# A graph network's sorting stage: node sums by wide matmuls, file copies by DMA, and all normed rows on ScalarE

## The reference

```python
x = _layernorm(x + _L0_gnn_ref(x, L0_gnn_W, L0_gnn_c, edge_index), axis=-1)
x = _layernorm(x + _L1_gnn_ref(x, src, dst, ...), axis=-1)
x = _layernorm(x + _L2_gnn_ref(x, edge_index, ...), axis=-1)
x = _layernorm(x + _L3_gnn_ref(x, edge_index, edge_attr_16, batch0, ...), axis=-1)
```

```python
f = h + EPS
f = f * CLIP / jnp.maximum(CLIP, _norm(f))
p = jnp.tanh(fn) * f / fn
Mp = p @ W
t = Mp * atan_norm / pn / sqrt_c
hh = jnp.tanh(sqrt_c * tn) / sqrt_c / tn * t
```

## Time and profile before

| | us |
|---|---|
| median of 3 runs | 8033.82 |
| lowest and highest | 8025.30, 8053.64 |
| the profiled execution | 8009.85 |
| its span in the trace | 8008.1 |

### The profile page before, as it was taken

The page is one execution under the profiler, slowest core; times in us unless marked ns, Lnnn a source line. Parts: engine busy times, 40 slices in busy tenths (PEclk is TensorE's granted clock), DMA queues, the critical chain, the costliest instruction groups (busy, mean ns, idle before and its releaser), DMA issues. The chain is left out here.

```text
span 8008.1 us, 79691 instructions
## 1 busy us (share of the span) xinstructions
PE 3054.5 (38%) x15477; PEld 2682.3 (33%) x15477; DVE 5462.4 (68%) x16234; ACT 2800.3 (35%) x6111; POOL 5534.3 (69%) x5455
## 2 busy tenths in 40 slices
PE   6999210211111116666656635455400000362322
PEld 4666210211111116666646634444400000252221
DVE  6677983877777756777779969999734443463764
ACT  2333550433333334444435536666500000121211
POOL 2442677777777767777757747777567777777677
PEclk8776555555555557878766655555555555576555
DMA  2343450111111114555469944444321111663321
GB/s 87 129 133 105 57 65 14 27 25 26 26 25 25 26 41 151 160 169 166 155 230 327 327 143 153 151 144 150 128 59 46 45 44 45 140 225 108 97 92 61
DMA packets 596808, 865.90 MB, mean 108 GB/s; under 512 B 267587, under 2 KB 281139, under 8 KB 590060
## 3 DMA queue, kind: packets, MB, share of 16 engines
q1 hardware_dynamic: 382812, 686.47, 26.0%
q0 software_dynamic: 163408, 175.42, 10.6%
q10 hardware_dynamic: 50240, 0.60, 0.6%
HBM read 393.46 MB, written 482.24 MB: 109 GB/s over the span
## 5 line engine op out<-in xcount | busy, mean ns | idle before, releaser
L2479 PE MATMUL e_turned<-ident,e_own_x 128*128 128x128 f32 x196 | 54.6, 434 | 1322.4 <-DVE e_own_x L2067 1322.4
L1340 POOL DMA_INDIRECT e_other<-X,index x392 | 436.1, 1112 | 171.1 <-issue 116.4
L1328 POOL DMA_INDIRECT e_ahead<-XA,index x392 | 413.5, 1055 | 178.8 <-issue 119.1
L3108 POOL DMA_INDIRECT e_got<-G,index x392 | 412.4, 1052 | 174.9 <-issue 113.3
L3730 POOL DMA_INDIRECT out_rows<-e4s_out,index x392 | 417.6, 1065 | 165.3 <-issue 118.8
L2000 POOL DMA_INDIRECT X<-e_row,index x392 | 420.4, 1073 | 124.1 <-issue 119.1
L164 POOL DMA_INDIRECT T<-slot_at,home_row x393 | 406.0, 1033 | 144.0 <-issue 142.1
L2628 POOL DMA_INDIRECT e_got<-X,index x392 | 412.1, 1051 | 119.5 <-issue 119.5
L2625 POOL DMA_INDIRECT e_mine<-X,index x392 | 401.7, 1025 | 130.4 <-issue 119.2
L3539 POOL DMA_INDIRECT rows<-X,index x392 | 397.1, 1013 | 131.5 <-issue 131.5
L1988 POOL DMA_INDIRECT e_mine<-T,index x392 | 394.4, 1006 | 127.7 <-issue 113.7
(11 more groups left out here) (704 smaller groups left out, 14101.7 us busy)
## 6 DMA issues: line engine op xcount, KB each, us to landing
XA<-e_n_xa SPq DMA_DIRECT2D x49, 1056.0 KB, 5.4
SUMS<-e_state SPq DMA_DIRECT2D x49, 1056.0 KB
e4n_n_xa<-XA SPq DMA_DIRECT2D x49, 1056.0 KB, 5.2
X<-e_n_row SPq DMA_DIRECT2D x49, 576.0 KB
T<-sort_filed SPq DMA_DIRECT2D x98, 280.0 KB
X<-pl_x SPq DMA_DIRECT2D x98, 268.0 KB, 3.3
e_n_x<-X SPq DMA_DIRECT2D x49, 536.0 KB
B<-e_n_b SPq DMA_DIRECT2D x49, 528.0 KB
```

The source lines that it names most:

```text
L1328: gp.indirect_dma_start(out=ahead[:, b, j, :], out_offset=None, in_=g.XA[0:SLOTS, :], in_offset=bass.IndirectOffsetOnAxis(ap=index_of(g, 0 ...
L1340: gp.indirect_dma_start(out=other[:, h, j, :], out_offset=None, in_=others[:, :], in_offset=bass.IndirectOffsetOnAxis(ap=index_of(g, s, 1, ...
L3108: gp.indirect_dma_start(out=got[:, h, j, :], out_offset=None, in_=g.G2[:, :], in_offset=bass.IndirectOffsetOnAxis(ap=index_of(g, s, 1, n, ...
```

## The change

Passes run at steps 0 and 2 of every five in the first order and at every second step of the second. The node sums are made by three matmuls of 512 columns with the small matrix as the stationary operand (`added`), copied out by ScalarE (`sums_out`), and transposed in four pieces (`nodes`). Each stage of a pass is asked for some steps later than before. GpSimd's copies for the file become loads by SyncE straight into the file tile; GpSimd only adds the node numbers. All 98 blocks of normed rows are made on ScalarE in halves; `by_vector` is False for all. The factors are made for 56 and 42 blocks. The diff, cut to its core:

```diff
-    pass_steps = [n for n in range(STEPS) if n % 3 != 2 and n + 1 not in turns][:CH]
+    pass_steps = [n for n in range(STEPS) if (n % 5 in (0, 2) if n < LENGTH else n % 2 == 0)][:CH]
     def batch_step(b):
-        return pass_steps[BATCH * b + BATCH - 1] + 5
+        return pass_steps[BATCH * b + BATCH - 1] + 9
-    def pool_norm_step(m):
-        return max(batch_step(m // BATCH) + 2, 30 + 7 * m // 4)
-    def act_norm_step(m):
-        return LENGTH + 8 + 5 * (m - POOLED) // 2
+    def norm_step(m):
+        if m < SOONER:
+            return max(batch_step(m // BATCH) + 2, 32 + 3 * m)
+        return LENGTH + 2 + 2 * (m - SOONER)
+    def by_vector(m):
+        return False
+    def filed_in(n):
+        return [m for m in range(CH) if 4 * m // 3 == n]
-    factor_starts = [max(batch_step(HALF // BATCH - 1) + 2, LENGTH + 2)]
+    halves = (range(0, FIRST_HALF), range(FIRST_HALF, CH))
+    factor_starts = [max(batch_step(FIRST_HALF // BATCH - 1) + 2, LENGTH + 2), batch_step(CH // BATCH - 1) + 2]
...
 SyncE
+                def file_in(m):
+                    h = m % 2
+                    sp.wait_ge(file_cleared, 1)
+                    if m >= 2:
+                        sp.wait_ge(filed_x[h], m // 2 * 16)
+                    rows = filed[:, h, :, 0:D]
+                    if m < CH - 1:
+                        sp.dma_start(rows, node_rows(x, m)).then_inc(file_loaded[h], 16)
...
+                def file_out(m):
+                    h = m % 2
+                    sp.wait_ge(numbers_made.sem, numbers_made.after(m))
+                    sp.wait_ge(file_loaded[h], (m // 2 + (2 if m == CH - 1 else 1)) * 16)
+                    sp.dma_start(chunk_rows(g.T0, m, W0), flat(filed[:, h, :, :])).then_inc(filed_x[h], 16)
...
-                for n in range(-8, STEPS):
-                    for m in passed(n + 2):
-                        file_x(m)
-                    for m in passed(n + 5):
+                for n in range(-8, STEPS + 8):
+                    for m in filed_in(n + 4):
+                        if m >= 1:
+                            file_out(m - 1)
+                        file_in(m)
+                    for m in passed(n + 8):
                         x_in(m)
+                    if n == CH * 4 // 3:
+                        file_out(CH - 1)
                     for m in normed(n + 6):
                         norm_rows_in(sp, m)
-                    for m in pool_normed(n - 1) + act_normed(n - 2):
+                    for m in normed(n - 2):
                         norm_rows_out(sp, m)
...
 GpSimd
-                    file_made.done(gp.tensor_copy(filed[:, m % 2, :, 0:D], xin[:, m % 4, :, :]), "rows")
-                    file_made.done(gp.tensor_scalar(filed[:, m % 2, :, W0 - 1], node_f[:, :], float(m * NODES), None, ALU.add), "node")
-                def norm_rows(m):
...
+                    numbers_made.done(gp.tensor_scalar(filed[:, m % 2, :, W0 - 1], node_f[:, :], float(m * NODES), None, ALU.add))
...
 TensorE
+                def added(m):
+                    t.wait_ge(squared.sem, squared.after(m))
+                    if m:
+                        t.wait_ge(sum_act.sem, sum_act.after(m - 1))
+                    for i, rows in enumerate((xt[:, m % 4, :], squares[:, m % 2, 0, :], squares[:, m % 2, 1, :])):
+                        last = t.matmul(summed[:, :], lhsT=g.stat[:, i, :, :].rearrange("p a k -> p (a k)"), rhs=rows, start=(i == 0), stop=(i == 2))
+                    sum_pe.done(last)
                 def nodes(m):
-                    t.wait_ge(squared.sem, squared.after(m))
+                    t.wait_ge(sum_act.sem, sum_act.after(m))
                     if m:
                         t.wait_ge(node_act.sem, node_act.after(m - 1))
                     for q in range(GROUP // 2):
-                        for i, rows in enumerate((xt[:, m % 4, :], squares[:, m % 2, 0, :], squares[:, m % 2, 1, :])):
-                            last = t.matmul(by_node[:, q, :], lhsT=rows[:, q * P:(q + 1) * P],
-                                            rhs=g.stat[:, i, :, :].rearrange("p a k -> p (a k)"), start=(i == 0), stop=(i == 2))
+                        last = t.transpose(by_node[:, q, :], sums[:, m % 2, q * P:(q + 1) * P], g.ident[0:2 * STATS, 0:2 * STATS])
                     node_pe.done(last)
...
-                    for m in passed(n - 1):
+                    for m in passed(n - 2):
                         projected(m)
+                    for m in passed(n - 5):
+                        added(m)
+                    for m in passed(n - 7):
+                        nodes(m)
                     for m in passed(n + 1):
                         turned_rows(m)
-                    for m in passed(n - 3):
-                        nodes(m)
...
 ScalarE
+                def sums_out(m):
+                    a.wait_ge(sum_pe.sem, sum_pe.after(m))
+                    if m >= 2:
+                        a.wait_ge(node_pe.sem, node_pe.after(m - 2))
+                    sum_act.done(a.activation(sums[:, m % 2, :], summed[:, :], ACT.Copy))
...
-                    for m in passed(n - 2):
+                    for m in passed(n - 8):
+                        nodes_out(m)
+                    for m in passed(n - 6):
+                        sums_out(m)
+                    for m in passed(n - 3):
                         squares_of(m)
-                    for m in passed(n - 4):
-                        nodes_out(m)
                     for b in batched(n):
                         batch_roots(b)
-                    for m in act_normed(n):
-                        norm_rows(m, 0, GROUP // 2)
-                    for m in act_normed(n - 1):
-                        norm_rows(m, GROUP // 2, GROUP)
                     if n in turns:
                         land_loads(n)
+                    for m in normed(n):
+                        if not by_vector(m):
+                            norm_rows(m, 0, GROUP // 2)
+                    for m in normed(n - 1):
+                        if not by_vector(m):
+                            norm_rows(m, GROUP // 2, GROUP)
```

More of the change, by code:

```diff
@@ L499, in order_edges @@
         scaled = Engine(sem("pl_scaled"), "inverse offset")
[L500 removed]
+        x1_act, x1_dve, halfway = (Step(sem(f"pl_{q}")) for q in ("x1_act", "x1_dve", "x1_halfway"))
         def after_norm(engine, m):
[L503 to L504 removed]
+            if by_vector(m):
+                engine.wait_ge(x1_dve.sem, x1_dve.after(vector_norms.index(m)))
             else:
[L506 removed]
+                engine.wait_ge(x1_act.sem, x1_act.after(scalar_norms.index(m)))
         def per_node(a):
@@ L825, in batch_scales, with norm_rows @@
                     scaled.done(v.tensor_tensor(offset[:, rows, :], centre[:, rows, :], inverse[:, rows, :], ALU.mult), "offset")
+                def norm_rows(m):
+                    h = m % 4
+                    v.wait_ge(scaled.sem, scaled.after(m // BATCH, "offset"))
+                    v.wait_ge(xr_loaded[h], rows_in(m))
+                    v.wait_ge(x1_stored[h], m // 4 * 16)
+                    v.wait_ge(x1_ones, 3)
+                    halfway.done(v.tensor_tensor(x1[:, h, :, 0:D], xr[:, h, :, :], per_node(inverse[:, m, :]), ALU.mult))
+                    v.wait_ge(halfway.sem, halfway.after(vector_norms.index(m)))
+                    x1_dve.done(v.tensor_tensor(x1[:, h, :, 0:D], x1[:, h, :, 0:D], per_node(offset[:, m, :]), ALU.add))
                 fa_done = acts_seen = 0
@@ L830, in factors @@
                     names = "n fs zeta a pn pc yn sp b t t2 u s sg".split()
-                    A = {q: work[:, i * HALF * GROUP:(i + 1) * HALF * GROUP] for i, q in enumerate(names)}
-                    rows = slice(half * HALF, (half + 1) * HALF)
+                    size = len(half) * GROUP
+                    A = {q: work[:, i * size:(i + 1) * size] for i, q in enumerate(names)}
+                    rows = slice(half[0], half[0] + len(half))
                     for i, q in enumerate(("nh2", "s1", "zs", "ez", "shift")):
@@ L981, in _ @@
                         batch_scales(b)
-                    for half in range(2):
-                        if n == factor_starts[half]:
-                            v.wait_ge(scaled.sem, scaled.after(HALF * (half + 1) // BATCH - 1, "offset"))
+                    for half, start in zip(halves, factor_starts):
+                        if n == start:
+                            v.wait_ge(scaled.sem, scaled.after(half[-1] // BATCH, "offset"))
                             factoring = factors(half)
-                        if 0 <= n - factor_starts[half] < SEGMENTS:
+                        if start <= n < start + SEGMENTS:
                             next(factoring)
-                        if n - factor_starts[half] == SEGMENTS:
+                        if n == start + SEGMENTS:
                             assert next(factoring, "end") == "end"
+                    for m in normed(n):
+                        if by_vector(m):
```

(1 more changed line is left out.)

72 lines of the change are left out of this document (28 added, 44 removed).

## The result

In runs shared with the kernel before, the changed kernel took 7765.1 us (median of four, 7758.4 to 7769.4) against 8029.6 us for the kernel before: a ratio of 0.967 with a 95% interval of 0.9641 to 0.9693, so 264 us or 3.3% sooner. A second set of five runs gave 7757.6 us against 8033.4, ratio 0.966 (0.9647 to 0.9674). The profiled execution took 7758.41 us (span 7756.7).

What follows compares the result with a forecast made beforehand. GpSimd's list of writes ends the stage, its start set by the first order, where VectorE waits behind ScalarE and ScalarE behind full TensorE. First order 490 us, list 212 us sooner: 8033.8 - 212 = 7822 us, range 7765 to 7975.

Steps and rivals of the forecast that it cites:

- the sum's terms for VectorE's waits: First order: VectorE waits 45 us for turned keys (bounds 12 to 74) and 40 for spare copies (22 to 110.9).
- the 490 taken: Forecast length of the first order's 136 steps in us, with 439 to 590 as bounds; 663.8 before.
- the clock of before: First order: TensorE's granted clock assumed to stay 0.72, making its work 453 us.
- the wide form does not save TensorE time: TensorE's cost of one pass at full clock: 5.42 us with wide sums against 4.86 before; the spreading saves time.
- (c): Rival, both orders: TensorE's clock falls as it works less, so the stage ends only 60 us sooner, 7974; chance 0.05.
- TensorE is still busy nearly throughout, so 45: First order: reason for taking 45 us, between 12 and 74, as VectorE's wait for turned keys.
- 28 heavy steps of 0.8: First order: 28 of 136 steps where ScalarE's 3.6 us of work stall VectorE by 0.8 us each, 22 us.
- GpSimd's stretching: First order: VectorE's sort instructions, lengthened beside GpSimd's elementwise work, give back 73.5 us when that work goes.
- Rival (d): Filing: 256-byte loads land slowly, 98 blocks take 1000 us, the list starts 256 us later, 8290; chance 0.07.
- Hidden with 18 us to spare: Stage's end: the second order's layout ends at 1128 us, before GpSimd's list of four-byte writes at 1146.
- rival (a): First order: TensorE, with ScalarE behind it, still sets the pace at 590 us; list 107 us sooner, 7927; chance 0.20.
- the lowest case: Low end of the range: a first order of 439 us saves 267 us in the list, giving 7767 us.

Runs made afterwards that it cites:

- a1_narrow: The changed kernel with the node sums of before (12 narrow matmuls a block), passes still spread; 7796.9 us, ratio 0.968 to 0.972.
- b2_spread: The kernel before with the changed kernel's pass spacing alone (55 blocks in the first order, 43 in the second); 8141.5 us.
- a8_first: The changed kernel with TensorE's turn of the next x rows put ahead of the projection in each step; 7748.5 us, ratio 0.962 to 0.9652.
- a3_pool: The changed kernel with idle work on GpSimd, two 128x512 multiplies for each filed block, results unread; 7860.0 us.

## Where the prediction was right, and where it failed

**Right: what bounds the stage, and the gain's place.** The list starts 1.1 us after the last `home_row` write; what came sooner is the first order (230.5 us) and the steps behind it, and the stage's end followed the list.

**Failed: the sum's terms for VectorE's waits**, 45 us for turned keys and 40 for spare copies, on a base that kept the 10.7 us of landed words. Measured: 25.5, 14.3 and 6.2, together 49.7 us less; the first order came out 56.7 below the 490 taken, and even below the lower bound of 439. Two things lie in it. First, the step "and the clock of before": with the wide form TensorE was granted 0.90, not 0.72, and the sentence "the wide form does not save TensorE time" holds only at equal clock. Its own count was good: 326 us at full clock, over 0.90, is 362 against 358.8 measured. a1_narrow, at a clock of 0.70, has waits of 68.9: 22.9 of the 49.7 us go with the form and its clock. None of the rivals had the clock rise; (c) had it fall. Second, the other 26.8: "TensorE is still busy nearly throughout, so 45" tied the wait to the engine's busy share. b2_spread, with TensorE busy 85% at 0.71, has waits of 45.6 in all, and a2_dense, the changed kernel with dense passes, is busy for only 76% and has 324.1 for the changed kernel's 46.0. So the busy share does not give the waits. What the runs show in its place is how closely the passes follow each other, and the order in which three queues stand behind each other: a8_first takes off 14 us by one line of it. (In the kernel before TensorE's load was a floor as well, as the prediction said.) Between the bounds for turned keys, 12 and 74, the lower row was the nearer one. For spare copies even the lower bound of 22 was too high: VectorE was stalled 19 times for 0.75 us on average, where the prediction had 28 heavy steps of 0.8.

**GpSimd's stretching: right.** 73.5 us forecast. VectorE's busy time fell by 80.8, but with eight instructions fewer; a2_dense, with the 743 of before, has 375.3 us for 450.4, so the stretching was 75.1. a3_pool shows the cause.

**After the first order: right.** 36.6 us from step 136 to `home_row` for 41.

**Filing by DMA: right.** The last `file_out` was issued at 486.8, the first load near 45: 4.5 us a block for 4.6, ahead of `home_row` by 54 us. Rival (d) needed 7.6. The landing of the 256-byte loads shows from above, since the store of a block waits for its load in SyncE's queue:

```profile
60.14 0.55 SPq L579 DMA_DIRECT2D sort_filed<-in_x  x1
...
63.75 0.33 SPq L588 DMA_DIRECT2D T<-sort_filed  x1
```

The store follows by 3.6 us here and at the median of all blocks, 3.2 at the least, so the 4 us taken were a little high, and so was the estimate of 4.0 by the Trainium skill's page ("DMA: Bandwidth & Descriptors", section Why small descriptors are slow).

**The list: 540 taken over, 550.6 measured.** Its last stretch of 143 us had a DMA share of 0.75, where the last 136 us of before had 0.06: the column stores now fall beside its end. That they cause the slower pace is argued from this, not shown, and it fits only half: 5.5 of the 10.8 us fall on the last quarter of the list, 3.1 on the first, where the DMA share was 0.29 for 0.34 before. The cause stays open.

**The second order: 537 forecast, 548.6 measured**, and its end was mis-sized. "About 10" for the late column stores was 31 us between the last step and the keys' issue: the stores left at 1.7 us each, near the 1.8 that it took, but they had backed up, since steps of 2.6 us ask for three of them. "Hidden with 18 us to spare" was false; the layout ended after the list, one of the prediction's own signs of being wrong, and held the next stage by 4.7 us. ScalarE also waited 38.1 us in this order for X1 stores, which stood in SyncE's queue among the 56 column stores of the first factor half (680 to 790 us), a term that the sum lacked.

**Sum of the misses.** The list started 61 us before the forecast (57 from the first order, 4 from the steps after it), and gave back 10.8 by its pace and 4.7 by the layout: about 46 more than forecast in the stage, 52 in the medians. (Two slips in the prediction's sums change no reading: by its own terms rival (a)'s list starts at 703, not 708, and the lowest case saves 263 us, not 267.)

## What to carry to other kernels

Where engines with hand-written orders pass work around, look for two things, the load of the fullest engine in the stretch and the ring (each one's next instruction behind the other's last). Spacing the passes was worth 166 us, of which at least 115 needed the load that it moved out; moving one line of TensorE's order was worth 74 us with dense passes and 15 with spread ones; the wide form, with some 30% more clock, 23 to 39. Write the sum as busy time of the engine that sets the pace plus its waits, bound each wait by the row of the least disturbed stretch, and ask of every engine whose work changes form whether its clock stays. Then look at what stands in a queue behind the last cheap stores of a stage.

## What the runs showed of the hardware

- In the first orders TensorE's granted clock went with the form of the matmuls and not with its busy share. With node sums of 10 columns it was 0.72, 0.71 and 0.70 at 92, 85 and 88% busy; with sums of 512 columns 0.95, 0.90 and 0.92 at 82, 83 and 76%. As a mix of its two levels (1.2 and 2.4 GHz), 0.70 is 40% of the time at full clock and 0.90 is 80%. In a later stretch with the wide form and less to do (744 to 1053 us, 42% busy) it was 0.68. Why was not tried.
- An elementwise instruction on GpSimd holds a VectorE compare to its own end: 1.26 us for 0.41. In a3_pool's first order 226 us of such work cost VectorE 115.
- Stores in 20-byte pieces leave SyncE at 1.7 us each, and while they drain the DMA engines' busy share is 1.29, that is full, at only 18 GB/s (1036 to 1083 us).
